# Attention beside routing: pieces per step from a table, gate product in column tiles, reciprocals on GpSimd

## The reference

```
mod = silu(c) @ wmod                    # six vectors per batch
h = layernorm(x) * (1 + ca) + sa
x = x + ga * (softmax(q k^T / 4) v @ w_o^T + b_o)
h = layernorm(x) * (1 + cb) + sb
scores = sigmoid(h @ gate^T)            # 32 experts
sfc = scores + bias; keep the 4 best of 8 groups, then the 6 best experts
tw = 2.5 * scores / sum(scores) over the picks
x = x + gb * (sum_e tw_e * expert_e(h) + shared(h))
```

## Time and profile before

| | us |
|---|---|
| median of 3 runs (1417.09 to 1418.15) | 1417.43 |
| the profiled execution | 1413.43 |
| its span | 1411.7 |
| attention steps, from the trace | about 150 to 882 |
| granted TensorE clock, mean over the span | 0.98 |

### The profile page before, as it was taken

The page is one execution under the profiler, slowest core; times in us unless marked ns, Lnnn a source line. Parts: engine busy times, 40 slices in busy tenths (PEclk is TensorE's granted clock), DMA queues, the critical chain, the costliest instruction groups (busy, mean ns, idle before and its releaser), DMA issues.

```text
span 1411.7 us, 30711 instructions
## 1 busy us (share of the span) xinstructions
PE 1345.3 (95%) x8191; PEld 672.9 (48%) x8192; DVE 1133.4 (80%) x2823; ACT 753.9 (53%) x1155; POOL 606.6 (43%) x782
## 2 busy tenths in 40 slices
PE   7997999999999999999999999999999999999895
PEld 4552222332333323323333232568788888888541
DVE  6886999999999999999999994565566656666588
ACT  3762477676767676776667768113334333343100
POOL 4000123133644534636347357527755555655300
PEclk9997799999999999999999999999999999999999
DMA  6897355533546445544464355937766665666698
GB/s 217 257 271 219 94 171 136 120 92 77 124 126 153 100 112 152 133 101 101 126 175 129 88 157 180 277 127 234 231 204 203 202 182 176 180 180 177 234 360 326
DMA packets 217021, 243.66 MB, mean 173 GB/s; under 512 B 94012, under 2 KB 181564, under 8 KB 216800
## 3 DMA queue, kind: packets, MB, share of 16 engines
q1 hardware_dynamic: 189392, 166.54, 43.7%
q0 software_dynamic: 21776, 68.07, 13.4%
q10 hardware_dynamic: 5760, 7.87, 1.7%
HBM read 133.98 MB, written 108.41 MB: 172 GB/s over the span
## 4 chain that ended last, share of the span: by engine, by line
PE 70%; DVE 13%; DMA 4%; issue 2%; POOL 1%; ACT 1%; SPq 0%; DVEq 0%; POOLq 0%
PE psO L1169 15%; PE psE L1156 13%; PE ex_psGU L1677 12%; PE psM L1146 10%; DVE piece_max L1043 9%; PE ex_psY L1692 6%; PE ex_psX L1666 3%; DMA wide<-results 2%; PE psM L505 2%; PE ex_psA L1686 2%; PE co_psS L1946 1%; PE psGU L1490 1%; DMA results<-vals_inv,places 1%; PE psM L524 1%; PE late_psGU L1926 1%
## 5 line engine op out<-in xcount | busy, mean ns | idle before, releaser
L1043 DVE TENSOR_REDUCE piece_max<-psM 128x1 f32<-128x512 f32 x1024 | 641.8, 680 | 25.8 <-PE psM L1146 22.4
L1110 ACT ACTIVATE wide<-psE 128x1024 f32<-128x1024 f32 x512 | 497.0, 1021 | 204.2 <-PE psE L1156 201.9
L1146 PE MATMUL psM<-wide 48*128 48x512 bf16 x1024 | 324.4, 395 | 20.2 <-DVE piece_max L1043 11.7
L1156 PE MATMUL psE<-wide 49*128 49x512 bf16 (+1 forms) x2048 | 329.8, 381 | 0.3
L1758 POOL DMA_INDIRECT results<-vals_inv,places x223 | 213.9, 959 | 150.2 <-DVE vals_inv L1744 84.7
L1169 PE MATMUL psO<-wide 128*32 128x512 f32 x2048 | 273.9, 607 | 0.6 <-ACT wide L1110 0.6
L1146 PEld LDWEIGHTS psM<-wide 48*128 48x128 bf16 x1024 | 78.1, 93 | 348.9 <-DVE piece_max L1043 276.9
L1677 PE MATMUL ex_psGU<-wide,ex_xT 128*128 x892 | 231.4, 382 | 0.7 <-ACT ex_xT L1709 0.7
L1156 PEld LDWEIGHTS psE<-wide 49*128 49x128 bf16 (+1 forms) x2048 | 117.9, 95 | 89.8 <-issue 9.3
L1677 PEld LDWEIGHTS ex_psGU<-wide,ex_xT 128*128 128x128 f32 x892 | 152.1, 190 | 14.9 <-issue 2.6
L1709 ACT ACTIVATE ex_xT<-ex_psX 128x256 f32<-128x256 f32 x223 | 85.3, 383 | 120.8 <-PE ex_psX L1666 119.8
(11 more groups left out here) (281 smaller groups left out, 1263.0 us busy)
## 6 DMA issues: line engine op xcount, KB each, us to landing
wide<-qk_parts SPq DMA_DIRECT2D x384, 64.0 KB
wide<-results SPq DMA_DIRECT2D x16, 1536.0 KB, 9.6
rows<-lists SPq DMA_DIRECT2D x112, 160.0 KB
h2Ts<-lists SPq DMA_DIRECT2D x111, 160.0 KB
qk_parts<-parts SPq DMA_DIRECT2D x32, 384.0 KB, 3.2
xin<-in_x_dram SPq DMA_DIRECT2D x16, 512.0 KB, 4.1
v_values<-vst SPq DMA_DIRECT2D x32, 256.0 KB, 3.6
wide<-v_values SPq DMA_DIRECT2D x16, 512.0 KB
```

The source lines that it names most:

```text
L1043: v.tensor_reduce(piece_max[:, qh, (x * PAIRS + h) * KT // QH + qt, kh:kh + 1], bank_of("piece", PIECES * group + n), AX.X, ALU.max, negat ...
L1110: nc.scalar.activation(probs[:, step % 2, 2 * pair:2 * pair + 2], psE[:, pair], ACT.Exp, scale=HD ** -0.5).then_inc(exp_ok, 1)
L1146: nc.tensor.matmul(bank_of(*user), qa[g][rows, h, qt * P:(qt + 1) * P], ka[g][rows, h, kh * 512:(kh + 1) * 512], start=True, stop=True).th ...
L1156: mm = nc.tensor.matmul(psE[:, pair, x], k[g][part, pair, kt * P:(kt + 1) * P], q[g][part, pair, qh * 512:(qh + 1) * 512], start=(q is qa) ...
```

## The change

The ring, VectorE's and TensorE's loops take the number of pieces of each step from a table. A step hosting projected rows has six, with the fifth and sixth issued inside and behind the projection; the transposition steps have five; w = 26, 27, 29, 30 have three and w = 28 has two. The order of the two row halves in the score products follows the parity of the piece number. The picks from d = 101 on move two places later. The gate product swaps its operands: 32 experts are the columns of the weights, and the four token tiles go to four column tiles of the array, so its result is turned (experts by tokens). ScalarE's tanh is kept; a new hosted product at w = 24 turns it back, and ScalarE instead of GpSimd writes 0.5 t + 0.5. GpSimd inverts the softmax sums (not those of the last group) with an integer first guess and three Newton rounds, in the middle of its written order and at the fourth scatter. SyncE stores and loads the maxima before it stores the inverse sums.

```diff
-PROJECT, TURN, GATE, PLACE = 11, 21, 23, 28
+PROJECT, TURN, GATE, SCORES, PLACE = 11, 21, 23, 24, 28
+PICK = 103
+SERVED = {PROJECT: 6, PROJECT + 1: 6, TURN: 5, TURN + 1: 5, 26: 3, 27: 3, 28: 2, 29: 3, 30: 3}
+def pieces_in(step):
+    return SERVED.get(step % WINDOW, 4) if step >= WINDOW else 4
...
 class Ring:
         for step in range(STEPS * B * NG):
-            for _ in range(4):
-                if n < total:
-                    take(("piece", n))
-                    n += 1
+            end = min(n + pieces_in(step), total)
+            early = min(n + 4, end)
+            for m in range(n, early):
+                take(("piece", m))
             c, w = divmod(step, WINDOW)
             if c and w in HOSTED:
                 take((c - 1, w))
+            for m in range(early, end):
+                take(("piece", m))
+            n = end
...
 def project_half(pe, env, c, half, to, after_tile=None):
...
-    mm.then_inc(env.projected, 1)
+        if i == TPC // 2 - 1:
+            mm.then_inc(env.projected, 1)
+        if after_tile:
+            after_tile(i)          # one piece behind each tile
...
+def gate_side_by_side(pe, env, c, to):
+    pe.wait_ge(env.h2T_ok, KC * (c + 1))
+    for k in range(KC):
+        for i in range(TPC):
+            mm = env.nc.tensor.matmul(to[E * i:E * i + E, 0:P], env.gate_w[:, k], env.h2T_of(c)[:, k, i * P:(i + 1) * P],
+                                      start=(k == 0), stop=(k == KC - 1))
+    mm.then_inc(env.gated, 1)
+def turn_scores(pe, env, c, to):
+    pe.wait_ge(env.bent_ok, c + 1)
+    env.nc.tensor.transpose(to[:, 0:P], env.bent[:], env.ident[:]).then_inc(env.scores_turned, 1)
+def scores_out(act, env, c, of):
+    act.wait_ge(env.scores_turned, c + 1)
+    wait(act, env.slot_read, c)
+    env.nc.scalar.activation(env.sc[:]..., of[:, 0:TPC * E], ACT.Copy, bias=0.5, scale=0.5).then_inc(env.sc_ok, 1)
...
 SyncE, finish_values:
                 if group + 1 < NGR:
-                    store_max(2 * group + 3)
+                    put_max(2 * group + 3)
                 store_inverse(group)
-                if group + 1 < NGR:
-                    load_max(2 * group + 3)
...
 GpSimd:
+            def inverse_sums(group):
+                bits, rest = inverse[:].bitcast(I32), env.act_s[0:HG * HD, 0, 0:S // HD]
+                pool.wait_ge(den_in, 16 * (group + 1))
+                wait(pool, inv_stored, 16 * group)
+                chain.link(g.tensor_scalar(bits, den[:].bitcast(I32), -1.0, float(FIRST_INVERSE), ALU.mult, ALU.add))
+                for n in range(ROUNDS):
+                    chain.link(g.tensor_tensor(rest, den[:], inverse[:], ALU.mult))
+                    chain.link(g.tensor_scalar(rest, rest, -1.0, 2.0, ALU.mult, ALU.add))
+                    ins = g.tensor_tensor(inverse[:], inverse[:], rest, ALU.mult)
+                    if n < ROUNDS - 1:
+                        chain.link(ins)
+                ins.then_inc(divided, 1)
...
             def scores(c):
-                pool.wait_ge(env.bent_ok, c + 1)
-                g.tensor_scalar(env.sc[:]..., env.bent[:], 0.5, 0.5, ALU.mult, ALU.add).then_inc(env.sc_ok, 1)
...
                     scatter_chunk(nc, env, c, n, n + 1)
+                    if n == DIVIDE:                      # now 3
+                        inverse_sums(2 * c + 3)
...
                     scatter_portion(c - 1, 2)
+                inverse_sums(2 * c + 2)
                 scores(c)
...
 VectorE, beside:
-                if n == 0 and step % STEPS == DIVIDE and step >= STEPS:
-                    divide(step // STEPS - 1)
-                    route_part(dve, env, steps, c, 4 * w + n, bank_of(c, w - 1))
+                    d = 4 * w + n
+                    if d < PICK - 2 or d >= PICK:
+                        route_part(dve, env, steps, c, d - 2 * (d >= PICK), bank_of(c, w - 1))
...
 TensorE, scores:
-                    for x in (0, 1) if pair == 0 else (1, 0):
+                    for x in (first % 2, 1 - first % 2):
...
 TensorE, loop over the steps:
+                first, end = pieces_for(step)
+                scores(step, g, s, 0, first)
+                piece(first, end)
+                scores(step, g, s, 1, first + 1)
+                piece(first + 1, end)
                 if step:
                     weighted_values(step - 1)
+                piece(first + 2, end)
+                piece(first + 3, end)
+                route_products(step, first + 4, end)
```

More of the change, by code:

```diff
@@ L61 @@
 FIRST_GUESS = 0x5F3759DF
+FIRST_INVERSE = 0x7EF311C7
 ROUNDS = 3
@@ L786, in bank_of @@
             return psM[:, ring.bank[user]] if user in ring.bank else None
+        first_piece = [HALF_PIECES + 4 * (AHEAD + step) for step in range(-AHEAD, 0)]
+        for n in itertools.accumulate((pieces_in(step) for step in range(ALL)), initial=HALF_PIECES + 4 * AHEAD):
+            first_piece.append(min(n, PIECES * NGR))
         def pieces_for(step):
-            return divmod(4 * (step + AHEAD + KT), PIECES)
+            return first_piece[step + AHEAD], first_piece[step + AHEAD + 1]
         @block.sync
@@ L1078, in _ @@
             for step in range(-AHEAD, ALL):
-                group, first = pieces_for(step)
-                for n in range(4):
-                    beside(step, n)
-                    if group < NGR:
-                        piece_maximum(group, first + n)
-                if group < NGR and (first + 4) % HALF_PIECES == 0:
-                    finish(QH * group + first // HALF_PIECES)
+                first, end = pieces_for(step)
+                for n in range(max(4, end - first)):
+                    if n < 4:
+                        beside(step, n)
+                    if first + n < end:
+                        piece_maximum(*divmod(first + n, PIECES))
+                        if (first + n + 1) % HALF_PIECES == 0:
+                            finish((first + n) // HALF_PIECES)
             env.divide_last = lambda: divide(NGR - 1)
@@ L1103, in beside @@
                     half_scores(act, env, c, bank_of(c, w))
+                if c >= 0 and pair == 1 and w == SCORES:
+                    scores_out(act, env, c, bank_of(c, w))
             for step in range(ALL):
@@ L1135, in bank_free, with piece @@
                     pe.wait_ge(env.bent_ok, c + 1)
+                elif w == SCORES:
+                    pe.wait_ge(env.sc_ok, c + 1)
                 else:
                     pe.wait_ge(env.placed_read, c + 1)
-            def piece(group, n):
+            def piece(number, end):
+                if number >= end:
+                    return
+                group, n = divmod(number, PIECES)
                 g = group % NG
-                user = "piece", PIECES * group + n
+                user = "piece", number
+                if n == 0:
+                    pe.wait_ge(loaded[g], 16 * LOADS * (group // NG + 1))
                 bank_free(user)
@@ L1148, in piece, with scores @@
                                  ).then_inc(piece_done, 1)
-            def scores(step, g, s, pair):
+            def scores(step, g, s, pair, first):
                 wait(pe, exp_ok, 2 * (step - 1) + pair + 1)
@@ L1171, in weighted_values, with route_products @@
                 mm.then_inc(summed, 1)
-            def route_products(step):
+            def route_products(step, more, end):
                 c, w = chunk_at(step)
@@ L1180, in route_products @@
                 if w in (PROJECT, PROJECT + 1):
-                    project_half(pe, env, c, w - PROJECT, to)
-                elif w in (TURN, TURN + 1):
+                    project_half(pe, env, c, w - PROJECT, to, lambda i: piece(more + i, end))
+                    return
+                if w in (TURN, TURN + 1):
                     turn_half(pe, env, c, w - TURN, to)
                 elif w == GATE:
-                    gate(pe, env, c, to)
+                    gate_side_by_side(pe, env, c, to)
+                elif w == SCORES:
+                    turn_scores(pe, env, c, to)
                 elif w == PLACE:
                     place(pe, env, c, to)
-            pe.wait_ge(loaded[0], 16 * LOADS)
+                piece(more, end)
             for n in range(HALF_PIECES + 4 * AHEAD):
-                piece(0, n)
+                piece(n, n + 1)
             for step in range(ALL):
```

32 lines of the change are left out of this document (12 added, 20 removed).

## The result

The changed kernel took 1429.82 us (median of six runs, 1427.45 to 1434.23), beside 1417.63 us (1414.01 to 1420.41) for the kernel before on the same chip. The ratio is 1.0094, with a 95% interval of 1.0075 to 1.0113; a later repetition gave 1.0089 [1.0068, 1.0111]. The prediction was 1412.1 us with a range up to 1422, so it was wrong in sign and outside its range.

What follows compares the result with a forecast made beforehand. VectorE and TensorE were taken as nearly even, VectorE bounding plain steps. Per window -0.43 + 3.2 - 1.0 - 2.85 = -1.1 us, -6.5 for six; with -0.4 and +1.6 at the ends, -5.3: 1412.1 us, range 1402 to 1422.

Steps and rivals of the forecast that it cites:

- I give back 0.9: ... 0.25 at w = 28, where the counts now wait for a selection made in the same step ... -2.85 us: Picks from w = 25: six pieces fewer save VectorE 3.7 us a window, less 0.9 for waits: -2.85 us, bounds -3.7 and -2.
- Following the ring, VectorE idles ... 1.35 against 3.09 ... -1.0 us with two pieces more: Turn to gate, w = 21 to 25: 12.7 us against 13.2 + 0.43 for the reciprocal, so -1.0 us a window.
- +3.2 us: Projected rows with six pieces: 558.27 against 555.03 per window, 2.5 of it pieces due anyway, the rest new waiting; range 2.5 to 4.7.
- The rival of pieces in series: Projected rows: pieces inside a full-array product run in series, 4.7 us in place of 3.2, giving 1422.6 us; chance 0.16.
- SyncE's new order: SyncE's queue: maxima stored at 604.7 instead of 603.85, there about 609.2, wanted at 609.8; rival with GpSimd late 1415 us, 0.15.
- the two reciprocals: VectorE at w = 5 and w = 21: each cost 0.43 us in a step VectorE bounds, so -0.43 each per window.
- the last window: Last window, where pieces run out at w = 20: +3.2 - 0.43 - 0.3 - 1.05 + 0.2 = +1.6 us.
- Window 0: First window: loses one reciprocal, -0.4 us.
- no stall at w = 0: First scores at w = 0 don't wait for the maxima; a wait before L1156 there would prove the prediction wrong.
- more levelling: Rival: new waiting at projected rows doesn't show (2.5 for 3.2), half the idle of 1.35 + 0.9 goes: 1401 us; chance 0.16.
- J1 to J2 over 6.5 us: Start of first projected half to second: about 6.0 us instead of 4.43; below 5.5 or above 6.5 means prediction wrong.
- no idle of more than 0.3 us in the picks: Sign of a right forecast in the profile after: VectorE idles no more than 0.3 us at once in the picks.

Runs made afterwards that it cites:

- each part alone: Kernel before with only the gate in column tiles, turn back and ScalarE's scores: 1409.62 us; with only GpSimd's reciprocals and SyncE's new order: 1408.97 us.
- both: Kernel before with gate tiles and GpSimd reciprocals together, four pieces in every step, picks in old places: 1403.63 us, repeated 1403.95 us.
- no shift: The changed kernel with the picks left in their old places: 1420.98 us, 1.0038 of the kernel before.
- pieces first, no shift: Changed kernel, picks in old places, fifth and sixth piece ahead of the projection on TensorE and in the ring: 1419.84 us, 1.0037 of the kernel before.
- two or three fifth pieces, no shift: Gate tiles and GpSimd reciprocals, four pieces at projected rows, old picks; fifth pieces at both turns: 1400.36 us; also at the gate: 1398.48 us.
- two fifth pieces with the shift: Gate tiles and GpSimd reciprocals, fifth pieces at both turns only, picks two places later: 1405.49 us, 0.9928 of the kernel before.
- the fastest: Gate tiles and GpSimd reciprocals, fifth pieces at both turns and the gate, picks in old places: 1398.48 us, 0.9881 of the kernel before.

## Why the prediction was wrong

The forecast was -5.3 us, and the windows gave +12.6. By its own steps, for six windows:

- **The step that failed most: "I give back 0.9: ... 0.25 at w = 28, where the counts now wait for a selection made in the same step ... -2.85 us".** Without the shift the term measures -2.67 us, with it -1.90 at full clock. The counts wait 1.77 us, where 0.25 was given back for it: VectorE had fewer maxima at w = 28 but all of the selection before it, and TensorE got there early. And the halved clock behind it, 1.04 us in four windows, was in no term. That is 6 x 0.95 and 4 x 1.04, 9.9 us in all. I had named what waits; I had not followed the two engines' times to that point.
- **"Following the ring, VectorE idles ... 1.35 against 3.09 ... -1.0 us with two pieces more"**, of which 0.43 was the reciprocal. Measured +0.06, and -0.3 in the section ahead, where that reciprocal stood. The gate came as predicted (-1.33 in its step), but the turn back took 0.60 instead of 0.15 to 0.3, the pieces behind it lying further apart, and the two fifth pieces cost 0.31 and 0.49 us: VectorE's idle time ahead of them mostly wasn't theirs to fill, 2.05 us of it stayed. That is 0.78 a window, 4.7 us.
- **"+3.2 us" at the projected rows** measured +3.7, 3 us over six windows. Order and wait were right (0.95 us before the next step's first piece); the tiles are 1.38 apart, and VectorE idles 0.69 between fifth and sixth piece. The rival of pieces in series asked for 4.7 and 0.68 us a piece; a piece inside the product costs 553.46 - 553.14 = 0.32, as forecast. It isn't the cause.
- **SyncE's new order** had been followed for the maxima only, and not for the inverse sums that now go behind them. It costs the projection 1.3 us once.
- Right, or nearly: the gate's 0.65 us, GpSimd's 3.6 us, the two reciprocals (-0.3 and -0.4 instead of -0.43), the last window (+2.1 instead of +1.6). VectorE's reads keep 0.62 us beside GpSimd's operations in SBUF (25 from 565.70 on in 15.50 us, with one of GpSimd's of 2.36 us at 576.77 among them). Window 0 was shorter by 0.8 us, not by 0.4. That there was no stall at w = 0 was luck in part: the maxima's load was 2.5 us later than reckoned, and TensorE was late as well.

The sum: 9.9 + 4.7 + 3 + 1.3 and 0.3 for the first reciprocal are 19.2. The window from 267 gives back 1.1, because only the kernel before had its clock drop there (94.23 against 93.05 in its others). The last window and window 0 differ from their terms by +0.5 and -0.4. That makes 18.2, for 12.6 + 5.3 = 17.9. A side sum was wrong too: 93 - 32 x 2.44 - 6 is 8.9 us, not 5; it only spoke for "more levelling". The rival "more levelling" was further off still. What I had named as marks of a wrong forecast, J1 to J2 over 6.5 us or a wait at w = 0, didn't appear, though it was wrong. Of the marks of a right one most held; "no idle of more than 0.3 us in the picks" failed, with 1.34, and the windows took 94.2 us and more instead of 92.0.

## What to carry to other kernels

Before moving work between steps, write down for each step which of the two engines ends it and by how much: moved work is free only up to the idle time of that one step, at its place in the order, so the first unit moved can be cheap (0.52 us here) and the second dear (1.33). When a producer is put later, take the time at which its consumer arrives, not the old gap, and count a wait of TensorE twice, once for itself and once for what the clock may do behind it. Try the parts of a change one by one; here the gate and the reciprocals were good, 0.8% together, and the shift and the sixth pieces hid it.

## What the runs showed of the hardware

- The granted clock can fall from 1.00 to 0.50 behind TensorE's wait for the counts, in the main the more often the longer that wait is, though these kernels differ in more than the wait. In the six full windows of each profile of the quicker sessions:

```
wait before the counts   kernels                                    windows   with a drop behind it
0.40 to 0.41 us          before, each part alone, both (twice)         30        2
0.58 to 0.59             no shift; pieces first, no shift              12        0
0.99                     two or three fifth pieces, no shift           12        3 (all with three)
1.02                     two fifth pieces with the shift                6        4
1.77                     the change (twice)                            12        8
```

  A drop lasts 3.4 us, twice in these profiles about twice that. Pieces first has three more at the projected rows, behind waits of 0.77 and 0.54 us. A window with one of 3.4 us is longer by 1.04 us in the changed kernel, 1.2 in the one before, 1.0 in the fastest, 1.6 in the one with pieces first and only 0.1 to 0.2 in that with two fifth pieces and the shift. What brings the drop about in one window and not in the next stays open.
- One full transposition of 128 columns costs its step 0.60 us, 0.33 by its record; scores and pieces behind it are 0.60 us apart instead of 0.44 for one round. The gate's sixteen products take 0.65 us in four column tiles of 32x128 outputs, where sixteen with 128x32 outputs took 1.97.
- GpSimd's ten operations on 64x64 took 0.24 (one input) and 0.32 us (two), about 0.36 from one to the next in a chain.
- The load of the inverse sums, issued at 446.60 ahead of 24 others, was there at about 455.4, nearly 9 us later. One issued at 351.81 was there by 357.24, since GpSimd didn't wait for it.
